# Queries and keys projected already transposed, in half-heads, in the attention part of a decoder layer

## The chip, the cores and the metric

The kernel runs on one core of a Trainium2 chip. The metric is the device time of one execution in microseconds. The kernel before takes 2218.97 us, the median of 3 runs (2217.65 to 2219.78).

## What is computed

A decoder layer on x of 16 batches, 256 positions, 512 features, in float32:

```python
x = x + attn(layernorm(x))      # 32 query heads of 64, 8 key/value heads, rotary
                                # embedding, causal window of 128, sinks, output projection
x = x + conv(ctx, ctx, layernorm(x))   # long convolution of k*v, 32 heads of 8 channels
x = x + mix(layernorm(x))       # sum of 8 factor matrices / sqrt(8), and a bias
```

Of the attention, what matters here:

```python
qkv = x @ qkv_w.T + qkv_b
q, k = rope(q), rope(k)         # [x1*cos - x2*sin, x2*cos + x1*sin], halves of 32
logits = einsum('bqhmd,bkhd->bhmqk', q, k) / 8     # masked: j > i or j <= i - 128
w = exp(logits - m) / (sum(exp(logits - m)) + exp(sink - m))
out = einsum('bhmqk,bkhd->bqhmd', w, v).reshape(...) @ out_w.T + out_b
```

## The kernel before, in words

Three parts follow each other: `attention_part`, `conv_part`, `mix_part`. Only the first is touched, with `rope_tables` and `layout`, which prepare its inputs.

The attention goes twice over the 16 batches, because the weights, each split in a high and a low float32r part so that three matmuls (high by high, low by high, high by low) stand for one in float32, fill SBUF for half of the key heads only. The first sweep takes key heads 0 to 3 and writes x plus its part of the output to DRAM (`part_dram`), the second takes 4 to 7, adds, and forms the second layernorm and its transpose (`q2_dram`) for the convolution. I call one batch in one sweep a window; there are 32. A window has eight slots: p % 4 names the key head (group), j the tile of 128 positions. A body is eight p's by two j's, so two windows; bodies 0, 1, 7, 8, 9, 15 and the drain 16 are written out, those between are loops. Nothing plans the order at run time: each engine's `body` issues its calls by p and j, with a lag for each stage, and semaphores tie the engines.

In slot (p, j), TensorE: transposes the four probability tiles of lag 3 into pP (`p_transposes`, L520); projects one tile of 128 positions onto the 384 columns of a group, queries, key and value together (`qkv`, L486, twelve matmuls into wP); transposes the rotated queries and keys of the slot two before (`q_transposes`, L496, three into tP); forms scores of two heads (`scores`, L510, heads of 64 rows in two halves of the array, into sP); probabilities by values (`pv`, L534, into vP); and the output projection of lag 5 (`out_projection`, L557, six matmuls of 512 columns into oP). Transposes of x (L465) and of the second layernorm (L566) share tP.

VectorE, in the order of its slot: `rotate` (L835, L836), the additions of the rotary embedding; `divide` (L861 to L869), which needs the exponentials of the slot before; `mask_transposed` (L878); `qkv_evac` (L826, L829), out of wP with the bias; `mask_min` (L846, L852), masks and row minimum of this slot's scores; low parts of x (`x_low`, L810) and of the output (`o_low`, L816); now and then layernorms and the residual (L893). ScalarE: `p_evac` (L657), `q_evac` (L636), `o_high` (L663), `exps` (L648, L651). POOL: the products of the rotary embedding (`cos_sin_parts`, L726, L730), the power for the layernorms (L720), the sinks (L740), without which L651 can't start, the bias to the residual (L764), and at the start the sum of the mix's factors by DMA (L770).

The split of the first sweep's weights goes with the start; that of the second's runs through body 0 and body 1 (L601, L924), its parts go to DRAM and are loaded at the turn between the sweeps. SP's queue carries all loads and stores in the order written.

Of the kernel before, what the change touches and what calls it, by code (L numbers as in the profile page):

```python
# [18 lines left out]
F32 = mybir.dt.float32  # L19
I32 = mybir.dt.int32  # L20
# [5 lines left out]
P = 128  # L26
# [7 lines left out]
GW = (QM + 2) * HD  # L34
RW = (QM + 1) * HD
SM_SCALE = 1.0 / math.sqrt(HD)
MASKED = 1.0e30
CHUNK = 2 * (QM + 2) * HD
# [12 lines left out]
def rope_tables():  # L51
# [14 lines left out]
    key = np.stack([np.concatenate([cos, cos], axis=1), np.concatenate([-sin, sin], axis=1)], axis=1)  # L66
    tab = np.stack([-SM_SCALE * key] * QM + [key], axis=2).astype(np.float32)
    return np.ascontiguousarray(tab.reshape(NT, P, 2 * (QM + 1) * HD).transpose(1, 0, 2))
# [18 lines left out]
def attention_part(nc, x, wqkv, bqkv, wout, bout, sinks, rope, masks, ident, factors, ssm_pad, dcoef,  # L87
                   x1_dram, q2_dram, pad_dram, fsum):

    part_dram = nc.dram_tensor("x_part_rows", [B, T, D], F32).ap()

    wq_dram = nc.dram_tensor("w_split", [GS, 2, P, KD * GW], F32).ap()
    xt_dram = nc.dram_tensor("xt_split", [B, 2, P, NT * KD * P], F32).ap()
    wo_dram = nc.dram_tensor("wo_split", [GS, 2, P, 2 * D], F32).ap()
    with ExitStack() as ctx:
# [8 lines left out]

        wh = sb("wh", [P, GS, KD, GW], F32R)
        wl = sb("wl", [P, GS, KD, GW], F32R)
        woh = sb("woh", [P, GS, 2, D], F32R)
        wol = sb("wol", [P, GS, 2, D], F32R)  # L120
        bias_sb = sb("bias_sb", [P, GS, GW])
        bo_sb = sb("bo_sb", [P, D])
        sink_sb = sb("sink_sb", [P, NH])
        rope_sb = sb("rope_sb", [P, NT, 2, QM + 1, HD])
# [4 lines left out]
        xTh = sb("xTh", [P, 2, NT, KD, P], F32R)  # L129
        xTl = sb("xTl", [P, 2, NT, KD, P], F32R)  # L130
# [5 lines left out]
        qk = sb("qk", [P, 2, QM + 1, HD])  # L136
        m1 = sb("m1", [P, 2, QM + 1, HD])
        m2 = sb("m2", [P, 2, QM + 1, HD])
        qr = sb("qr", [P, 2, QM + 2, HD])
        vv = sb("vv", [P, NKV, NT, HD])  # L140
        qT = sb("qT", [P, 2, 3, T])
# [5 lines left out]
        pT = sb("pT", [P, 2, 2, SK])  # L147
        den = sb("den", [P, 4, 2 * NT])
        rden = sb("rden", [P, 4, 2 * NT])
        oTh = sb("oTh", [P, 4, NT, 2, P], F32R)  # L150
        oTl = sb("oTl", [P, 4, NT, 2, P], F32R)
        xb = sb("xb", [P, NT, D])
        x1 = sb("x1", [P, NT, D])
        work = sb("work", [P, 3 * CHUNK])
        x1n = work[:, 0:NT * D].rearrange("p (t d) -> p t d", t=NT)
        x1T = work[:, NT * D:2 * NT * D].rearrange("p (c t) -> p c t", c=KD)
# [77 lines left out]
        def chunks(gs):  # L234
            return [("qkv", g, i) for g in gs for i in range(2)] + [("out", g, i) for g in gs for i in range(2)]
# [1173 lines left out]
```

## Time and profile before

| | us |
|---|---|
| median of 3 runs | 2218.97 (2217.65 to 2219.78) |
| the profiled execution, its own time | 2217.66 |
| its span | 2215.5 |
| TensorE busy | 2086.6 (94%) |
| VectorE busy | 1753.5 (79%) |
| ScalarE busy | 929.9 (42%) |
| POOL busy | 835.2 (38%) |
| attention, to the first transfer of the convolution | 1721.1 |

The span is from the first to the last instruction of the program. Busy times are unions over an engine's instructions; a matmul's recorded duration holds the way through the array, so that matmuls overlap in the record and the distance between two starts, not the duration, tells what one costs. Where a row of VectorE ends later than the next begins, the same holds.

### The profile page before, as it was taken

To read this page: it belongs to the slowest core of one execution; us is meant where nothing else is said; L and a number is where in the kernel's file an instruction comes from. 1 tells how busy PE (TensorE), PEld (TensorE's weight loads), DVE (VectorE), ACT (ScalarE), POOL (GpSimd) and SP (SyncE) were. 2 spreads that over 40 slices of the span, in tenths; PEclk is the share of its full clock that TensorE was granted. 3 is DMA by queue.
4 is the path that set the end of the run, shared out by engine and by line. 5 is a ranking of instruction groups with operands and counts; after the bars stand their busy time and mean duration, and the time that the engine had idled before them with its cause. 6 is when DMAs were issued, how large, how long until landed. Compare 5 with 4: busy or idle time off the path is not lost. (4 is left out here: it accounts for less than half of the span.)

```text
span 2215.5 us, 45127 instructions
## 1 busy us (share of the span) xinstructions
PE 2086.6 (94%) x12672; PEld 1656.8 (75%) x12672; DVE 1753.5 (79%) x6468; ACT 929.9 (42%) x3429; POOL 835.2 (38%) x1327
## 2 busy tenths in 40 slices
PE   5669999999999999999999999999998699999699
PEld 4557888888888888887777777777875577676587
DVE  6558887878888887777777787778776599999787
ACT  3334444444444444444444444444443122222233
POOL 3223333333344333333333333333331355454354
PEclk9889999999999999999999999999999899999899
DMA  7663111111111114311121111111101633233364
GB/s 232 187 188 116 49 61 55 64 60 48 48 48 48 48 65 180 115 39 49 50 76 49 49 48 49 61 54 48 49 30 48 231 84 90 83 91 83 111 219 160
DMA packets 84765, 191.72 MB, mean 87 GB/s; under 512 B 7777, under 2 KB 20833, under 8 KB 84465
## 3 DMA queue, kind: packets, MB, share of 16 engines
q1 hardware_dynamic: 72112, 157.67, 21.6%
q10 hardware_dynamic: 8640, 23.86, 2.9%
q0 software_dynamic: 3840, 8.39, 2.1%
q14 instruction: 126, 1.02, 0.1%
q8 instruction: 47, 0.77, 0.1%
HBM read 120.68 MB, written 60.90 MB: 82 GB/s over the span
## 5 line engine op out<-in xcount | busy, mean ns | idle before, releaser
L726 POOL TENSOR_TENSOR m<-qk,rope_sb 128x320 f32<-128x320 f32 x256 | 223.3, 872 | 956.9 <-DVE qk L826 956.9
L648 ACT ACTIVATE pr<-pr,mx 128x128 f32<-128x128 f32 x1024 | 399.3, 391 | 222.1 <-DVE mx L852 222.1
L486 PE MATMUL wP<-wh,xTh 128*128 128x384 f32 x1024 | 373.4, 365 | 10.5 <-DVE vv L829 10.5
L1091 PE MATMUL y<-kv,tap 128*128 128x288 f32 x1280 | 330.3, 414 | 27.3 <-DVE res L1139 9.6
L486 PE MATMUL wP<-wh,xTl 128*128 128x384 f32 x1024 | 353.3, 345 | 0.0
L486 PE MATMUL wP<-wl,xTh 128*128 128x384 f32 x1024 | 350.8, 343 | 0.0
L1091 PEld LDWEIGHTS y<-kv,tap 128*128 128x128 f32 x1280 | 240.6, 192 | 116.9 <-issue 25.1
L730 POOL TENSOR_TENSOR m<-qk,rope_sb 128x160 f32<-128x160 f32 x512 | 260.3, 530 | 0.0
L510 PE MATMUL sP<-qT 64*128 64x128 f32 (+1 forms) x2048 | 237.1, 350 | 1.0 <-DVE mx L852 1.0
L636 ACT COPY qT<-tP 128x384 f32<-128x384 f32 x256 | 122.6, 479 | 272.4 <-PE tP L496 272.0
L852 DVE CUSTOM_DVE_ANT_0 pr<-sP,mask_sb 128x128 f32<-128x128 f32 x1024 | 235.1, 284 | 0.7
L869 DVE TENSOR_SCALAR pr<-pr,rden 128x128 f32<-128x128 f32 x1024 | 224.0, 282 | 9.1
L557 PE MATMUL oP<-woh,oTh 128*128 128x512 f32 x512 | 229.6, 448 | 0.0
L534 PE MATMUL vP<-pT,vv 128*64 128x256 f32 (+1 forms) x2048 | 223.6, 339 | 0.4 <-DVE oTl L816 0.4
L1041 POOL TENSOR_TENSOR kv<-kk 128x1024 f32<-128x1024 f32 x64 | 144.1, 2251 | 182.8 <-PE y L1091 158.5
L534 PEld LDWEIGHTS vP<-pT,vv 128*64 128x64 f32 x2048 | 124.5, 136 | 115.5 <-issue 73.8
L486 PEld LDWEIGHTS wP<-wh,xTh 128*128 128x128 f32 x1024 | 197.6, 193 | 13.7 <-issue 11.8
L557 PE MATMUL oP<-wol,oTh 128*128 128x512 f32 x512 | 203.2, 397 | 0.0
L557 PE MATMUL oP<-woh,oTl 128*128 128x512 f32 x512 | 201.4, 393 | 0.0
L520 PE MATMUL pP<-id_sb,pr 128*128 128x128 f32 x1024 | 157.5, 277 | 45.4 <-DVE pT L878 42.3
L486 PEld LDWEIGHTS wP<-wh,xTl 128*128 128x128 f32 x1024 | 197.9, 193 | 0.0
L486 PEld LDWEIGHTS wP<-wl,xTh 128*128 128x128 f32 x1024 | 196.7, 192 | 0.0
(93 smaller groups left out, 3594.2 us busy)
## 6 DMA issues: line engine op xcount, KB each, us to landing
tap<-padded_taps SPq DMA_DIRECT2D x64, 256.0 KB, 3.4
kk<-in_ctxt SPq DMA_DIRECT2D x64, 192.0 KB, 3.1
x_in<-in_x SPq DMA_DIRECT2D x16, 512.0 KB, 4.9
fsum<-in_factors POOLq DMA_DIRECT2D x8, 1024.0 KB, 9.6
xb<-in_x SPq DMA_DIRECT2D x16, 512.0 KB, 4.3
xt_split<-xTh SPq DMA_DIRECT2D x16, 512.0 KB, 2.6
xt_split<-xTl SPq DMA_DIRECT2D x16, 512.0 KB, 3.7
x_part_rows<-x SPq DMA_DIRECT2D x16, 512.0 KB, 3.1
```

Source lines behind the costliest of these rows:

```text
L486: last = pe.matmul(wP[:, 0:GW], a[:, p // 4, j, c, :], w[:, g, c, :], start=(c == 0 and n == 0), stop=(c == KD - 1 and n == 2))
L510: last = pe.matmul(sP[:, a, k0:P + 2 * k0], qT[r, s, j, t * P:(t + 1) * P], qT[r, s, 2, 0:(t + 1) * P], start=True, stop=True)
L520: last = pe.transpose(pP[:, (2 * a + t) * P:(2 * a + t + 1) * P], pr[:, (2 * p + 2 + j) % 4, a, t * P:(t + 1) * P], id_sb[:])
L534: last = pe.matmul(vP[a * HD:(a + 1) * HD, k * P:T], vu[:, k, :], pT[:, s, a, 2 * k * P:2 * P + k * P], start=(k == 0), stop=(k == 1))
L557: last = pe.matmul(oP[j][:], a[:, (p - 5) % 4, j, c, :], w[:, g, c, :], start=(g == 0 and c == 0 and n == 0), stop=(g == GS - 1 and c == 1 ...
L648: act.activation(pr[:, s, a, cols], pr[:, s, a, cols], ACT.Exp, bias=mx[:, s, i:i + 1], scale=-1.0, accum_out=ac[:, s, i:i + 1])
L726: pool.tensor_tensor(m1[:, j], qk[:, j], rope_sb[:, j, 0], ALU.mult)
L730: last = pool.tensor_tensor(m2[:, j, :, d:d + half], qk[:, j, :, o:o + half], rope_sb[:, j, 1, :, d:d + half], ALU.mult)
L852: last = dve.tensor_tensor_reduce(pr[:, s, a, t * P:(t + 1) * P], sP[:, a, 2 * t * P:(2 * t + 1) * P], mask_sb[:, t * P:(t + 1) * P], 1.0, ...
L869: last = dve.tensor_scalar(pr[:, s, a, cols], pr[:, s, a, cols], rden[:, s, i:i + 1], None, ALU.mult)
L1041: pool.tensor_tensor(kv[:, s, :, 0:4 * n].rearrange("p c (d n) -> p c d n", d=4), k0.unsqueeze(2).broadcast_to([P, KD, 4, n]), shifted, AL ...
L1091: last = pe.matmul(y[:, s, c, 0:NY], tap[:, s, d * P:(d + 1) * P], kv[:, s, c - d, :], start=(d == 0), stop=(d == c))
```

## The change

Queries, keys and values of four key heads are projected in six units per window instead of eight calls per window: five units (`unit`, L499) hold the weights still and stream x, so that the result comes out transposed, 128 rows being one half (32 numbers) of four heads, 256 columns being the positions; one unit (L492) makes the values of all four heads. Units stand in slots 0, 1, 3, 5, 6 and 7. The transposes of queries and keys go, with tP.

VectorE multiplies each unit out of PSUM with cosine and sine, adding the bias on the way (`turned`, L791, four instructions of 128x256); POOL adds the two products (`rotate`, L700) into qT or kT. Scores are formed for one query head of each of four key heads at a time, in four groups of 32 rows, two half-heads accumulated (L514), once per p. A row of four heads is now one query head of each key head, and weights and sinks are reordered for it. The output projection runs in a window of its own, one to two windows behind, one tile after the other, into one bank (L560). The residual comes in slots 3 and 7. The second sweep's weights are split at the turn, out of DRAM into the places of the first's, ten chunks of 1024 columns (L610, L781), without going through DRAM. The factors are summed in body 1 instead of body 0. The buffer `work` goes; x_in and xn take its uses.

On TensorE, a slot with j = 0 in the loop of the first sweep; names in it are the tiles of the lists above, an `x2` counts instructions. Before, from the end of the projection on:

```order
L486 MATMUL wP<-wl,xTh 128x384
L496 MATMUL tP<-id_sb,qr 128x128 x3
L510 MATMUL sP<-qT 128x128 x2
L510 MATMUL sP<-qT 128x256 x2
L534 MATMUL vP<-pT,vv 64x256 x2
L534 MATMUL vP<-pT,vv 64x128 x2
L557 MATMUL oP<-woh,oTh 128x512
```

and with the change, from the end of a unit on:

```order
L499 MATMUL wP<-xTh,wl 128x256
L514 MATMUL sP<-kT,qT 128x128 x8
L514 MATMUL sP<-kT,qT 128x256 x8
L538 MATMUL vP<-pT,vv 64x256 x2
L538 MATMUL vP<-pT,vv 64x128 x2
L560 MATMUL oP<-woh,oTh 128x512
```

The transposes between projection and scores are gone; the scores of two slots stand together, in four times as many matmuls.

On VectorE, from one minimum to the next mask. Before, in a slot in which a low part of x follows:

```order
L852 ISA mx 128x1
L816 TENSOR_TENSOR oTl<-vP,oTh 128x2x128
L835 TENSOR_TENSOR qr<-m 128x256
L836 TENSOR_TENSOR qr<-m 128x128
L861 TENSOR_TENSOR den<-ac,es 128x4
L863 RECIPROCAL rden<-den 128x4
L869 TENSOR_SCALAR pr<-pr,rden 128x128 x4
L878 TENSOR_TENSOR pT<-pP,mask_sb 128x2x256
L826 TENSOR_TENSOR qk<-wP,bias_sb 128x320
L829 TENSOR_TENSOR vv<-wP,bias_sb 128x64
L846 COPY_PREDICATED sP<-mask_sb,sP 128x2x128
```

and with the change, at the turn, with a split in it:

```order
L815 ISA mx 128x1
L850 TENSOR_TENSOR oTl<-vP,oTh 128x256
L781 TENSOR_TENSOR wl<-x_in,wh 128x1024
L824 TENSOR_TENSOR den<-ac,es 128x4
L826 RECIPROCAL rden<-den 128x4
L832 TENSOR_SCALAR pr<-pr,rden 128x128 x4
L841 TENSOR_TENSOR pT<-pP,mask_sb 128x2x256
L791 SCALAR_TENSOR_TENSOR m<-wP,bqk_sb,rope_sb 128x256 x4
L809 COPY_PREDICATED sP<-mask_sb,sP 128x2x128
```

The additions left the stretch ahead of the division, and four instructions of 128x256 stand where two smaller ones stood, between the masked transposes and the next mask. The diff, cut:

```diff
...
@@ TensorE
+                steps = [(wh, xTh), (wh, xTl), (wl, xTh)]
+                if n == V_UNIT:
...
+                    for h in range(2):
+                        for c in range(KD):
+                            for i, (w, a) in enumerate(steps):
+                                last = pe.matmul(wP[:, h * T:(h + 1) * T], w[:, n, c, h * P:(h + 1) * P], a[:, s, c, :],
+                                                 start=(c == 0 and i == 0), stop=(c == KD - 1 and i == 2))
+                    last.then_inc(qk_done, 1)
...
-            def q_transposes(y, p, j):
...
                 for t in range(NT):
-                    for a in range(2):
-                        r = slice(a * HD, a * HD + HD)
-                        k0 = t * P
-                        last = pe.matmul(sP[:, a, k0:P + 2 * k0], qT[r, s, j, t * P:(t + 1) * P],
-                                         qT[r, s, 2, 0:(t + 1) * P], start=True, stop=True)
+                    for h in range(2):
+                        for r in range(GS):
+                            rr = slice(r * 32, r * 32 + 32)
+                            last = pe.matmul(sP[:, r, t * P:P + 2 * t * P], qT[rr, p % 2, h, t * P:(t + 1) * P],
+                                             kT[rr, kslot, h, 0:(t + 1) * P], start=(h == 0), stop=(h == 1))
...
                         if x_next(y, p, j):
+                            x_transposes(y.window(p) + 1, p % 4 - 1)
+                        elif x1_here(y, p, j):
...
+                        if j == 0 and y.here(p, 2):
+                            scores(y, p)
...
@@ POOL
-            def cos_sin_parts(y, p, j):
...
+                pool.tensor_tensor(dst, m1[:, s], m2[:, s], ALU.add).then_inc(qr_ready, 1)
...
@@ VectorE
+            def turned(y, p, i):
...
+                for dst, h, half, f in [(m1, 0, 0, 0), (m1, 1, 1, 0), (m2, 0, 1, 1), (m2, 1, 0, 2)]:
+                    last = dve.scalar_tensor_tensor(dst[:, s, h], wP[:, half * T:(half + 1) * T], bias[:, half:half + 1],
+                                                    tab[:, f], ALU.add, ALU.mult)
...
-                        u, jj = (p - 1, 1) if j == 0 else (p, 0)
-                        if y.here(u, 0):
-                            rotate(y, u, jj)
...
+                        if residual_tile(y, p, j) is not None:
+                            residual(y, p, residual_tile(y, p, j))
+                        n = unit_of(p, j)
...
+                                turned(y, p, rope_index(n))
+                        if x_next(y, p, j):
+                            x_low(y.window(p) + 1, (p // 4 + 1) % 2, p % 4 - 1)
                         if y.here(p, 2):
                             mask_min(y, p, j)
...
+                        for i, n in split_now(y, p, j):
+                            split_low(i, n)
...
```

## Rows read from the trace of the kernel before

**Rows 1.** Windows: stretch, length, busy us of each engine (instructions), granted clock, DMA.

```profile
191.60:792.60 601.00, 599.82 (x4010) 483.04 (x4009) 503.83 (x2150) 287.58 (x1175) 237.48 (x420) 1.00 0.17 57
```

**Rows 2.** Windows of L861 alone, one division per slot, counted by its x.

```profile
45.40:191.60 146.20, 2.47 (x16) 0.85 0.65 179
191.60:792.60 601.00, 16.30 (x96) 1.00 0.17 57
...
1092.10:1503.30 411.20, 10.33 (x64) 1.00 0.15 52
```

**Rows 3.** Timeline of TensorE, one slot: start us, duration us, instruction, count.

```profile
599.98 0.49 PE L496 MATMUL tP<-id_sb,qr 128*128 128x128 f32 x3
600.39 0.93 PE L510 MATMUL sP<-qT 64*128 64x128 f32 x8
601.25 0.87 PE L534 MATMUL vP<-pT,vv 128*64 128x256 f32 x8
...
602.62 0.39 PE L557 MATMUL oP<-wol,oTh 128*128 128x512 f32 x1
602.85 0.39 PE L557 MATMUL oP<-woh,oTh 128*128 128x512 f32 x1
...
604.35 0.33 PE L486 MATMUL wP<-wl,xTh 128*128 128x384 f32 x1
604.52 0.34 PE L486 MATMUL wP<-wh,xTh 128*128 128x384 f32 x1
...
606.10 0.27 PE L496 MATMUL tP<-id_sb,qr 128*128 128x128 f32 x1
```

**Rows 4.** Timeline of VectorE in the drain, from one division to the next.

```profile
1691.78 0.16 DVE L861 TENSOR_TENSOR den<-ac,es 128x4 f32<-128x4 f32 x1 [1.20 <-ACT es L651]
...
1692.98 0.68 DVE L878 TENSOR_TENSOR pT<-pP,mask_sb 128x512 f32<-128x512 f32 x1
1693.58 0.42 DVE L846 COPY_PREDICATED sP<-mask_sb,sP 128x256 f32<-128x256 int32 x1
...
1694.75 0.08 DVE L852 DVE_READ_ACCUMULATOR2_ANT mx<- 128x1 f32 x1
...
1696.65 0.16 DVE L861 TENSOR_TENSOR den<-ac,es 128x4 f32<-128x4 f32 x1 [0.56 <-ACT es L651]
```

**Rows 5.** Timeline of VectorE, an instruction out of PSUM and its follower.

```profile
602.67 0.42 DVE L816 TENSOR_TENSOR oTl<-vP,oTh 128x256 fp32r<-128x256 f32 x1
603.01 0.41 DVE L835 TENSOR_TENSOR qr<-m 128x256 f32<-128x256 f32 x1
```

**Rows 6.** Timeline, a division held by POOL's power.

```profile
615.38 0.08 DVE L852 DVE_READ_ACCUMULATOR2_ANT mx<- 128x1 f32 x1
...
618.94 0.16 DVE L861 TENSOR_TENSOR den<-ac,es 128x4 f32<-128x4 f32 x1 [0.80 <-ACT es L651]
```

**Rows 7.** Timeline, a division held by POOL's additions to xb.

```profile
609.10 2.73 POOL L764 TENSOR_TENSOR xb<-xb,bo_sb 128x512 f32<-128x512 f32 x2
...
610.59 1.39 DVE L836 TENSOR_TENSOR qr<-m 128x128 f32<-128x128 f32 x1
...
611.90 0.15 DVE L861 TENSOR_TENSOR den<-ac,es 128x4 f32<-128x4 f32 x1
```

**Rows 8.** Timeline of TensorE and windows, an idle stretch and the clock behind it.

```profile
123.86 0.45 PE L520 MATMUL pP<-id_sb,pr 128*128 128x128 f32 x1 [3.45 <-DVE pT L878]
...
123.50:127.00 3.50, 3.14 (x12) 3.17 (x13) 2.25 (x13) 1.55 (x8) 2.81 (x5) 0.54 0.63 201
```

**Rows 9.** Timeline of body 0, a low part of the second sweep's weights, and one cast.

```profile
64.80 0.96 DVE L924 TENSOR_TENSOR work<-work 128x768 fp32r<-128x768 f32 x1 [8.67 <-ACT work L601]
...
71.47 0.81 ACT L601 CAST work<-work 128x768 fp32r<-128x768 f32 x1
```

**Rows 10.** Timeline of SP, the convolution's first transfer.

```profile
1721.12 0.35 SPq L1023 DMA_DIRECT2D kk<-in_ctxt  x1
```

**Rows 11.** The page, costliest groups: count | busy us, mean ns of one.

```profile
L486 PEld LDWEIGHTS wP<-wh,xTl 128*128 128x128 f32 x1024 | 197.9, 193 | 0.0
```

More of the change, by code:

```diff
@@ new lines, in x1_transposes, with unit_free @@
+            def x1_transposes(r, t, roped):
+                n = 2 * (r - B) + t
+                pe.wait_ge(x1n_ready, n + 1)
+                pe.wait_ge(m_ready, roped)
+                wait(pe, x1t_evac, n)
+                for c in range(KD):
+                    last = pe.transpose(wP[:, c * P:(c + 1) * P], x1n[:, t, c * P:(c + 1) * P], id_sb[:])
+                last.then_inc(x1t_done, 1)
+            def unit_free(y, p, n):
+                v = y.window(p)
+                if n == 5:
+                    pe.wait_ge(v_ready, v + 1)
+                elif n == 0:
+                    wait(pe, m_ready, (QM + 1) * v)
+                else:
+                    pe.wait_ge(m_ready, (QM + 1) * v + n)
+                if n in (2, 3):
+                    if fresh(y, p):
+                        pe.wait_ge(xt_lo, 2 * v + n + 1)
+                    elif late(y, 3, p):
+                        pe.wait_ge(x1t_evac, 2 * (v - 3 - B) + n - 1)
@@ L551, in out_projection @@
-                if g == 0:
-                    wait(pe, x1_ready, 4 * y.m + 2 * ((p - 5) // 4) - 1 + j)
-                steps = [(oTh, woh), (oTl, woh), (oTh, wol)]
-                for c in range(2):
-                    for n, (a, w) in enumerate(steps):
-                        last = pe.matmul(oP[j][:], a[:, (p - 5) % 4, j, c, :], w[:, g, c, :],
-                                         start=(g == 0 and c == 0 and n == 0), stop=(g == GS - 1 and c == 1 and n == 2))
-                last.then_inc(out_done, 1)
@@ new lines, in out_projection, with out_here @@
+                if k == 0:
+                    wait(pe, x1_ready, 2 * v + t)
+                steps = [(oTh, woh), (oTl, woh), (oTh, wol)]
+                for c in (2 * k, 2 * k + 1):
+                    for n, (a, w) in enumerate(steps):
+                        last = pe.matmul(oP[:], a[:, o, c, t * P:(t + 1) * P], w[:, c, :],
+                                         start=(c == 0 and n == 0), stop=(c == NO - 1 and n == 2))
+                last.then_inc(out_done, 1)
+            def out_here(y, p, j):
+                last_slot = p % 4 == 3 and j == 1
+                if y.first:
+                    return p == 7 and j == 1
+                return not (y.drain and p == 7 and j == 1)
@@ L573, in body @@
+            for t in range(NT):
+                x_transposes(0, t)
             def body(y):
@@ L1351, in _, with decoder_layer @@
             steps(dve, body, lag=4)
[L1354 removed]
+def decoder_layer(nc, x, ctxt, wqkv, bqk, bv, wout, bout, sinks, ssm_pad, dcoef, factors, bias, rope, masks, ident, out):
     x1_dram = nc.dram_tensor("x1_rows", [B, T, D], F32).ap()
```

768 lines of the change are left out of this document (356 added, 412 removed).

## Prediction

> **What bounds the kernel now.** I read a table of windows first, then one slot on TensorE, then the drain. The reader is to see that TensorE is busy 599.8 of 601.0 us in the first sweep [rows 1]. VectorE's divisions (L861, one per slot) count the slots: 96 in 601.0 us and 64 in 411.2 us [rows 2]. Eight slots make a window, so a window takes 50.1 us in the first sweep and 51.4 in the second. The first 16 take 146.2 us, against 100 at the steady pace.
>
> One slot on TensorE [rows 3] runs from 599.98 to 606.10, 6.12 us, of which three query transposes take 0.41 and the scores 0.86. TensorE is the bound, but hardly: behind it lies a ring over VectorE and ScalarE. The exponentials of a slot need its mask and minimum (L852), the next slot's division needs them, and VectorE works in order, so that the next mask comes behind that division. The drain, where no projection is left, shows the bare ring [rows 4]: from one division to the next 4.87 us, of which 1.82 pass between the last minimum (1694.83) and the division, 1.20 are the division, 0.60 the masked transposes, 1.25 the mask and minimum.
>
> **The change part by part, TensorE.** Query transposes go: 0.41 x 8 = 3.3 us per window. Scores go from eight calls of 0.86 to four. One now does four rounds (two half-heads, two tiles); a matmul of 128 columns is two records of 0.107 us and one of 256 two of 0.218, worked out of those 0.86 (2 x 0.107 + 2 x 0.218 + 0.2 of filling and of changing shape). If four row groups run beside each other as two do now, four rounds are 1.3 + 0.2 = 1.5 us, 6.0 per window against 6.9; if only two do, 2.8 us, 11.2 per window. I take the four, for the eight records of now already show pairs beside each other.
>
> Projections keep their columns but become 144 matmuls of 256 instead of 96 of 384. The pitch is 0.17 us at 384 columns and 0.23 at 512 [rows 3]: columns at 2.4 GHz (0.160, 0.213) and some 0.016. For 256 that makes 0.123. The bounds are 0.107, the columns alone, and 0.175, no gain from fewer columns; the three transposes, each with a weight load and 0.107 apart by the records' lengths above, speak for the low side. So 17.7 us against 16.8. The output projection keeps its 48 matmuls. TensorE's sum per window: 49.0 + 1.1 (transposes of x) - 3.3 - 0.9 + 0.9 = 46.8, about 46.5 with four changes of shape fewer.
>
> **VectorE and its ring.** Out go the evacuation (0.52 per slot in the ring: 0.40 and 0.12) and the rotation's additions. Those lay while ScalarE did the exponentials, so their removal frees nothing. In comes, in five of eight slots and in the ring between masked transposes and mask, L791: four instructions of 128x256 out of PSUM. The nearest is L816, same size and also out of PSUM, 0.42 long, the next starting 0.34 after it [rows 5]; 4 x 0.34 = 1.35 us. The lower bound is 0.26 each, what 256 more elements add from L816 to the 128x512 of L878, also out of PSUM (0.60 to the next start [rows 4]), the upper 0.42 with no overlap: 1.0 to 1.7. The value unit costs 0.60, as L878. Two residual tiles (0.60 each) now stand before the mask instead of under the exponentials, so do the two low parts of x in the first sweep (0.60 each), and the second layernorm's start in the second (1.7).
>
> Two waits of POOL remain in the ring in the first sweep. The power for x's layernorm stands ahead of the sinks in POOL's queue: the division came 3.48 us after the minimum, 1.66 over the 1.82 [rows 6]. And while POOL adds the bias to xb (two adds, 2.73 us), VectorE's two-input instructions from SBUF stand still: L836 took 1.39, and the division came at 611.90, 3.03 after its minimum, 1.2 over the 1.82 [rows 7]. The new POOL addition of 128x512 (half of those 2.73) runs beside the mask and minimum, which come out of PSUM, and costs nothing; without that cover it would hold the division by its own length.
>
> Window, first sweep: 8 x 4.87 + 5 x 1.35 + 0.6 + 1.2 + 1.2 + 1.66 + 1.2 = **51.6**. Second: 8 x 4.87 + 5 x 1.35 + 0.6 + 1.2 + 1.7 = **49.2**, taken as 49.4, since TensorE is held once by VectorE's long last slot. Both stand above TensorE's 46.5: the ring becomes the bound, and most of what TensorE saves is lost. TensorE now idles. In slot 2 of a window of the first sweep it waits some 3 us for the normalised x, which comes only after slot 1's minimum. After such a gap, of 3.45 us, the granted clock of the next 3.5 us was 0.54 [rows 8], the lower level. Transposes and scores right behind it take 2 us longer, of which half fits in: + 0.9, so **52.5** in the first sweep.
>
> **Start, turn, end.** At the start each slot waited for the second sweep's weights, which went from DRAM through a split and out again: L924 once stood 8.67 us for its cast [rows 9]. These leave, and so does the summing of the factors by DMA, now in slots 16 to 31: 1 MB in two slots, 12.9 us, is 81 GB/s more than the sweep's 57 [rows 1], below the start's 179 [rows 2], so I take it as hidden. New, estimated: the first projection starts at some 13 us; 5 us at the lower clock, 1.4 for L791, 3.0 for the next unit, then on VectorE five splits (6), L791 twice (2.7), a layernorm (2.7), low parts (1.2), mask (1.3) and the exponentials (1.8) make the first division at about 39 us instead of 45.5. Three slots of some 8.4 with a split in each follow, then 8 of 6.1 and five of 6.8. The 17th division comes at about 147 instead of 191.7: **-45**. A split costs a slot 2.2 us: its cast on ScalarE (1.05 for 1024 elements, by the 0.81 of 768) comes behind the exponentials, VectorE's 1.14 after that (0.96 for 768, less the overlap), and only then the division. In SP's queue the turn's ten loads stand, each behind the split before, ahead of the store of x1 and the load of xb. Those have four slots, some 25 us, until VectorE asks for them in slot 3, so I put them at nothing; if a split came late, SP and with it the residual would wait as long.
>
> From there to the last division, before, 1505 us (191.7 to 1696.65). Now: 107 slots of the first sweep, 13.4 x 52.5 = 702, - 3 for the last window without an x, + 5 splits 11; 16 x 49.4 = 790, + 5 splits 11, - 3 for windows without a second layernorm; drain 25. Sum 1533: **+28**. End: the last minimum to the first transfer of the convolution was 26.3 us (1694.83 to 1721.12 [rows 10]); the output projection now lags by up to 11 slots instead of five, five calls of 1.5 less what already stood there: **+5**. Convolution and mix are not touched.
>
> -45 + 28 + 5 = -12. The profiled execution took 2217.7 us (span 2215.5), 1.3 below the median of the runs, 2219.0. So **2206 us**.
>
> **One rule against the trace.** The 0.39 us matmuls stand 0.23 apart and those of 384 columns 0.17 [rows 3], though each has a weight load, 0.193 on record [rows 11]: the loads are hidden. The Trainium skill (TensorE: Matmul & The Clock Gate, section The mechanism) says that a weight load overlaps matmuls in flight only where the row group differs. By that rule the trace does not agree: here the loads and the matmuls have the same full height and yet follow each other at the pitch of their columns. By the rows the sum stays 2206, by the rule it would be the 2464 of the rival below.
>
> **Rivals.**
> *TensorE stays the bound through small matmuls (ends slower).* Place: L492 and L499. At the other end of the bounds, 0.175 instead of 0.123, a window needs 46.5 + 7.5 = 54.0 us. It decides from 0.143 in the second sweep (49.4) and from 0.16 in the first. Result: 29.4 windows, + 1.5 x 13.4 + 4.6 x 16 = + 94: about 2300. *Exposed weight loads (slower still).* With each load, as long as the 128 columns of a transpose (0.107), ahead of its matmul instead of beside the one before, 144 x 0.214 make a window of 59.6 and a time of 2464. Against it: 384 columns and such a load would be 0.267 apart, and are 0.17. It is the rule of the page named above.
> *Scores run two at a time* (the change doesn't do what it says): + 5.2 per window on TensorE, 51.7: bound in the second sweep, + 2.3 x 16 = 37, late scores in the first + 10: 2253.
> *The start gives nothing or half,* because transfers are late behind each other in SP's queue, or the ring meets waits that I don't see: 2225 to 2250.
> *The ring is shorter than its rows say,* since instructions overlap more or the start gains more: 2150 to 2190. For: the ring stands on 1.82 us that ScalarE might cut. Against: its four exponentials have the same form after.
>
> **How the numbers follow.** What a measurement tells from no change is 0.2%, 4.4 us about 2219. Chances: ring as computed, 2185 to 2225, 0.56; small matmuls 0.10; exposed loads 0.02; scores in pairs 0.06; start or unseen waits 0.14; shorter ring 0.12. Faster: the last, and three quarters of the first, 0.54. Same (2214.5 to 2223.4): 0.13. Slower: 0.33. The range leaves out the upper half of the small-matmul case and the lower part of the short ring: 2165 to 2285.
>
> **What would show it.** Right: divisions 4.9 apart in slots without a unit and 6.2 in those with one; TensorE idle 8 to 12% in the sweeps, its waits ended by VectorE; VectorE's division ended by ScalarE nearly always; L499 pitch near 0.123; scores near 1.5 us; 17th division near 147 us. Wrong: TensorE without gaps (small matmuls or scores), or L791 over 0.42 us, or slots with waits for DMA.

## The result and the profile after

The changed kernel takes 2263.35 us (median of 4 runs, 2262.38 to 2264.49) against 2218.56 before (4 runs): ratio 1.0202, 95% interval 1.0184 to 1.0219. It is 2% slower. The forecast was 2206, faster, with a chance of 0.54 for faster and 0.33 for slower; the time lies in the range given, on the side of the smaller chance.

From the page of the changed kernel: the span, TensorE's and VectorE's busy time, then two of VectorE's groups (busy us, mean ns | idle time before them and what ended it).

```profile
span 2260.6 us, 48490 instructions
...
PE 2029.4 (90%) x15488; PEld 1634.3 (72%) x15488; DVE 1720.5 (76%) x6104; ACT 803.9 (36%) x3161; POOL 557.6 (25%) x719
...
L824 DVE TENSOR_TENSOR den<-ac,es 128x4 f32<-128x4 f32 x256 | 52.7, 206 | 343.9 <-ACT es L632 314.7
L791 DVE SCALAR_TENSOR_TENSOR m<-wP,bqk_sb,rope_sb 128x256 f32<-128x256 f32 x640 | 264.4, 476 | 19.5 <-PE wP L499 18.8
```

TensorE is busy 90% of the span. VectorE's division L824 stood 343.9 us idle before it, 314.7 of them until ScalarE's last exponential. By these waits the ring over VectorE and ScalarE is the bound, as forecast (E1 to E3 test it). What came out otherwise is its length.

VectorE's divisions in the stretches of the forecast, as in [rows 2] (stretch and length, busy us of the divisions and their number, granted clock, DMA share, GB/s); each stretch begins just before the division that opens it:

```profile
46.30:154.45 108.15, 3.40 (x16) 0.91 0.22 63
154.45:880.80 726.35, 26.05 (x107) 0.96 0.22 64
880.80:1709.50 828.70, 22.47 (x128) 0.99 0.15 51
```

| stretch | before | forecast | now |
|---|---|---|---|
| to the first division | 45.5 | 39 | 46.4 |
| first to 17th | 146.2 | 108 | 108.1 |
| 17th to 124th | | 710 | 726.4 |
| 124th to 252nd | | 798 | 828.7 |
| 252nd to last (256th) | | 25 | 20.1 |
| 17th to last | 1505.0 | 1533 | 1575.2 |
| last division to the span's end | 518.9 | 523.9 | 530.9 |

So 37 us were won at the start, 70 lost between the 17th and the last division, 12 at the end: +45.

One slot on VectorE, the last of a window (slot 7) in the first sweep, to be read against the drain's bare one [rows 4] (start, length, engine, line, operation):

```profile
600.43 0.16 DVE L824 TENSOR_TENSOR den<-ac,es 128x4 f32<-128x4 f32 x1 [1.48 <-ACT es L632]
...
601.63 0.69 DVE L841 TENSOR_TENSOR pT<-pP,mask_sb 128x512 f32<-128x512 f32 x1
602.24 0.68 DVE L863 TENSOR_TENSOR x<-oP,xb 128x512 f32<-128x512 f32 x1
602.83 1.65 DVE L791 SCALAR_TENSOR_TENSOR m<-wP,bqk_sb,rope_sb 128x256 f32<-128x256 f32 x4
604.40 0.42 DVE L809 COPY_PREDICATED sP<-mask_sb,sP 128x256 f32<-128x256 int32 x1
...
605.57 0.42 DVE L850 TENSOR_TENSOR oTl<-vP,oTh 128x256 fp32r<-128x256 f32 x1
607.47 0.16 DVE L824 TENSOR_TENSOR den<-ac,es 128x4 f32<-128x4 f32 x1 [1.48 <-ACT es L632]
```

From division to division 7.04 us, where the drain has 4.87: the residual takes 0.59 (602.24 to 602.83) and L791's four products 1.57 (602.83 to 604.40), all of it between the masked transposes and the mask. Then the same wait of 1.48 us for the exponentials. By such rows a window of the first sweep is 7.97 + 6.44 + 5.47 + 7.85 + 5.47 + 6.44 + 5.47 + 7.04 = 52.15 us (slots 0 to 7) and one of the second 6.44 + 6.44 + 4.87 + 7.03 + 4.87 + 6.44 + 5.47 + 9.13 = 50.7; forecast were 51.6 and 49.2. On top, slot 2 of the first sweep took up to 6.75, and eight slots took 1.9 to 2.5 us beyond these.

These eight are where the two loops of five bodies branch back. VectorE's waits up to the last division (in total, times, longest), then one such place: VectorE's last row before the branch and first behind it, and ScalarE's exponentials of the sinks, which the division waits for.

```profile
DVE den L824 <- ACT es L632: 314.7, 234, 1.5
DVE den L824 <- issue: 29.2, 8, 3.9
```
```profile
1294.93 0.42 DVE L850 TENSOR_TENSOR oTl<-vP,oTh 128x256 fp32r<-128x256 f32 x1
1298.70 0.16 DVE L824 TENSOR_TENSOR den<-ac,es 128x4 f32<-128x4 f32 x1 [3.35 <-issue]
```
```profile
1296.60 0.19 ACT L632 ACTIVATE es<-sk 128x4 f32<-128x4 f32 x1
```

The exponentials are there at 1296.79 (1296.60 + 0.19), the division starts at 1298.70, 1.9 us later, with nothing on record that held it. At the eight branches back it was late by 2.11, 2.06, 2.30, 2.11, 2.27, 1.91, 2.49 and 2.46 us, 17.7 in all; everywhere else in a steady window the difference is 0.02 to 0.04.

### The profile page after: what moved, and what is told of

Read it like the earlier page. It is cut to its first block and busy times, and to the rows that moved or that the text cites. A ratio compares the mean times of both kernels' runs of the same rounds, so it can differ in the third digit from the quotient of the medians.

```text
span 2260.6 us, 48490 instructions
## 1 busy us (share of the span) xinstructions
PE 2029.4 (90%) x15488; PEld 1634.3 (72%) x15488; DVE 1720.5 (76%) x6104; ACT 803.9 (36%) x3161; POOL 557.6 (25%) x719
## 3 DMA queue, kind: packets, MB, share of 16 engines
q8 instruction: 129, 2.11, 0.4%
## 5 line engine op out<-in xcount | busy, mean ns | idle before, releaser
L499 PE MATMUL wP<-xTh,wh 128*128 128x256 f32 x1280 | 382.5, 299 | 20.8 <-DVE m L791 16.9
L499 PE MATMUL wP<-xTl,wh 128*128 128x256 f32 x1280 | 368.3, 288 | 0.0
L499 PE MATMUL wP<-xTh,wl 128*128 128x256 f32 x1280 | 367.1, 287 | 0.0
L700 POOL TENSOR_TENSOR qT<-m 128x512 f32<-128x512 f32 x128 | 164.8, 1287 | 690.9 <-DVE m L791 690.9
L824 DVE TENSOR_TENSOR den<-ac,es 128x4 f32<-128x4 f32 x256 | 52.7, 206 | 343.9 <-ACT es L632 314.7
L791 DVE SCALAR_TENSOR_TENSOR m<-wP,bqk_sb,rope_sb 128x256 f32<-128x256 f32 x640 | 264.4, 476 | 19.5 <-PE wP L499 18.8
L499 PEld LDWEIGHTS wP<-xTh,wh 128*128 128x128 f32 x1280 | 250.6, 196 | 26.7 <-DVE m L791 11.3
L560 PE MATMUL oP<-woh,oTh 128*128 128x512 f32 x512 | 231.2, 451 | 34.6 <-DVE x L863 34.4
L499 PEld LDWEIGHTS wP<-xTl,wh 128*128 128x128 f32 x1280 | 250.8, 196 | 0.0
L499 PEld LDWEIGHTS wP<-xTh,wl 128*128 128x128 f32 x1280 | 250.4, 196 | 0.0
L514 PE MATMUL sP<-kT,qT 32*128 32x128 f32 (+1 forms) x4096 | 221.5, 356 | 20.0 <-DVE mx L815 19.8
L560 PE MATMUL oP<-wol,oTh 128*128 128x512 f32 x512 | 204.1, 399 | 0.0
L560 PE MATMUL oP<-woh,oTl 128*128 128x512 f32 x512 | 204.0, 398 | 0.0
L514 PEld LDWEIGHTS sP<-kT,qT 32*128 32x128 f32 x4096 | 162.6, 199 | 47.0 <-issue 20.2
```

Of the source, the lines that this page charges most:

```text
L499: last = pe.matmul(wP[:, h * T:(h + 1) * T], w[:, n, c, h * P:(h + 1) * P], a[:, s, c, :], start=(c == 0 and i == 0), stop=(c == KD - 1 an ...
L514: last = pe.matmul(sP[:, r, t * P:P + 2 * t * P], qT[rr, p % 2, h, t * P:(t + 1) * P], kT[rr, kslot, h, 0:(t + 1) * P], start=(h == 0), st ...
L560: last = pe.matmul(oP[:], a[:, o, c, t * P:(t + 1) * P], w[:, c, :], start=(c == 0 and n == 0), stop=(c == NO - 1 and n == 2))
L700: pool.tensor_tensor(dst, m1[:, s], m2[:, s], ALU.add).then_inc(qr_ready, 1)
L791: last = dve.scalar_tensor_tensor(dst[:, s, h], wP[:, half * T:(half + 1) * T], bias[:, half:half + 1], tab[:, f], ALU.add, ALU.mult)
```

## The experiments

All times are medians, set against the changed kernel's 2263.35 unless said otherwise. Each kernel is the changed one but for the edit shown.

### E1 and E2: more work on VectorE, inside the ring and outside

```diff
 # E1, in turned()
+                last = dve.scalar_tensor_tensor(spare[:, s], wP[:, 0:T], bias[:, 0:1], tab[:, 2], ALU.add, ALU.mult)
                 last.then_inc(m_ready, 1)
 # E2, in o_low(), behind the masks
+                for i in range(2):
+                    dve.tensor_tensor(spare[:, j, i], vP[:, 0:T], oTh[:, (u // 4) % 2, c].bitcast(F32), ALU.subtract)
```

> One product more of the rotation (L791's form, 128x256 from PSUM, into a spare tile) in each of the five query and key units of a window, ahead of the masks as the others are. Ring theory (VectorE and ScalarE hand the same slot to each other, and the rotation stands inside that ring): every one costs its start to start of 0.39 us, 160 units = about +62 us against the changed kernel's 2263, so 2325, and the slots with a unit of queries or keys grow from 6.44 to 6.83. TensorE theory (its own work sets the pace): within 10 us of 2263.

> Two 128x256 subtractions more in every slot (256 slots, 0.34 us each, 174 us of VectorE work in all), put behind the masks, where VectorE waits for the exponentials. Ring theory: hidden in a wait of 1.2 to 1.5 us; only slot 0 of a window of sweep 1, where the layernorm's power and with it the sinks come later, pays some 0.7, so 0 to +12 us: 2263 to 2275. Theory that VectorE is full (its sum of work is the bound): +120 to +174 us. TensorE theory: within 10 us of 2263, so that this run alone does not tell it from the ring.

E1: 2322.94 us, **+60** for 160 instructions, 0.37 each; its unit slots are 6.83 us. E2: 2286.80, **+23** for 512 instructions. So an instruction ahead of the masks costs all but its full distance of 0.39, one behind them 0.05. VectorE's sum of work is not the bound; the place is. E2 was dearer than expected (up to 12): at the 113th division it is 24.8 us behind, at the 241st 26.6, so the first sweep pays nearly all of it. There slot 0 is 8.63 instead of 7.97 (as expected, the layernorm and its power come later), and slot 2 up to 7.4 instead of 6.75: TensorE idles 3.5 to 4.4 us in slot 1 instead of 2.1 to 3.0, and in 11 of 12 windows the granted clock of slot 2 is 0.58 to 0.78.

### E3: less work on TensorE

```diff
-                steps = [(wh, xTh), (wh, xTl), (wl, xTh)]
+                steps = [(wh, xTh), (wh, xTl)]
```

> Leaves out the third pass of the projection of queries, keys and values (low weights times high x): 48 of the 144 products of a window, so the outputs lack the low part of the weights. TensorE has 5.8 us less in each of 32 windows. Ring theory: the pace does not change; only at the eight loop-backs, where TensorE comes late, and at the start may 5 to 20 us go: 2243 to 2260. TensorE theory: -5.8 x 32 = -186 us, 2080.

2253.48 us, **-10**, of which 4.2 are the first division (42.2 instead of 46.4). The five looped bodies of the first sweep, of the changed kernel and of E3 (columns: stretch and its length, busy us of TensorE, its weight loads, VectorE, ScalarE, GpSimd, granted clock, DMA share, GB/s):

```profile
260.60:802.90 542.30, 492.99 (x4242) 403.44 (x4240) 408.31 (x1680) 201.73 (x901) 109.94 (x160) 0.96 0.14 49
```
```profile
256.70:794.40 537.70, 450.15 (x3760) 350.63 (x3760) 407.37 (x1681) 200.03 (x901) 110.01 (x160) 0.93 0.15 49
```

TensorE sheds 42.8 us of busy time (492.99 to 450.15) and the stretch 4.6. The granted clock fell too, 0.96 to 0.93, which lengthens what is left. TensorE does not set the pace: that theory asked for -186.

### E7: the sinks ahead of the layernorm's power

GpSimd's two steps change places in the program; nothing else.

> GpSimd takes the sinks ahead of the layernorm's power in the slot in which it has both; nothing else. Ring theory: slot 0 of every window of sweep 1 goes from 7.97 to 6.44 us (as in sweep 2, where there is no such power): 15 x 1.5 = -23 us, 2238 to 2245. If the slot is held by TensorE: 2263.

2240.18 us, **-23**. Slot 0 of the first sweep is 6.65 instead of 7.97, but for two slots behind a branch back, and slot 2, up to 6.75 in the changed kernel, is 5.46 to 5.91. Of the forecast's term for this wait, 1.66, slot 0 gives back 1.3 (it stood 1.5 over the 6.44 of the second sweep).

### E8 and E10: no branches back

```diff
-            with eng.Fori(2, HM - 1) as m:
+            for m in range(2, HM - 1):
                 body(Body(m, 0))
```
and the same for the second loop, in the changed kernel (E8) and in the kernel before (E10).

> The two loops of five bodies written out, so that no engine branches back. At each of the eight branches back VectorE's division came 1.9 to 2.5 us after its exponential sum, and in sweep 1 TensorE was late behind it by another 0 to 4 us. If the branch is the cause: -8 x 2.2 - 8 = -18 to -27 us, 2236 to 2246. If it is something else that falls at the end of a body (a layernorm, a DMA): 2263.

> The kernel before the change with its two loops of five bodies written out. Theory that the branch back was there all along: its looped bodies took 100.4 and 102.8 us, the written-out ones beside them 98.4 and 101.1, so 8 x 1.8 = -14 us, 2202 to 2208. Theory that only the changed kernel pays for it (a longer body): 2219.

E8: 2235.98 us, **-27**, the far end of what was expected (24.3 between the two profiled executions). Its bodies 2 to 6 all take 105.8 to 105.9 us (106.0 to 111.7 with the loop), bodies 10 to 13 of the second sweep 101.2 to 101.6 (103.7 to 104.0): besides VectorE's 17.7 us, TensorE came late behind the branch in the first sweep (slot 0 there takes up to 11.98 instead of 7.97). E10: 2216.93 against 2219.07, ratio 0.9992 (0.9983 to 1.0002): **nothing**. My reading of the longer looped bodies of before as the branch's price was wrong. The divisions of before around one branch back in the second sweep, then the same ones written out:

```profile
1257.08 0.16 DVE L861 TENSOR_TENSOR den<-ac,es 128x4 f32<-128x4 f32 x1 [0.68 <-ACT es L651]
...
1268.33 0.15 DVE L861 TENSOR_TENSOR den<-ac,es 128x4 f32<-128x4 f32 x1
...
1273.72 0.16 DVE L861 TENSOR_TENSOR den<-ac,es 128x4 f32<-128x4 f32 x1 [0.44 <-ACT es L651]
...
1279.12 0.16 DVE L861 TENSOR_TENSOR den<-ac,es 128x4 f32<-128x4 f32 x1 [0.35 <-ACT es L651]
...
1286.88 0.16 DVE L861 TENSOR_TENSOR den<-ac,es 128x4 f32<-128x4 f32 x1 [0.78 <-ACT es L651]
...
1292.29 0.15 DVE L861 TENSOR_TENSOR den<-ac,es 128x4 f32<-128x4 f32 x1
```
```profile
1257.23 0.16 DVE L861 TENSOR_TENSOR den<-ac,es 128x4 f32<-128x4 f32 x1 [0.68 <-ACT es L651]
...
1265.08 0.16 DVE L861 TENSOR_TENSOR den<-ac,es 128x4 f32<-128x4 f32 x1 [0.94 <-ACT es L651]
...
1271.22 0.16 DVE L861 TENSOR_TENSOR den<-ac,es 128x4 f32<-128x4 f32 x1 [0.94 <-ACT es L651]
...
1277.35 0.16 DVE L861 TENSOR_TENSOR den<-ac,es 128x4 f32<-128x4 f32 x1 [0.35 <-ACT es L651]
...
1285.86 0.16 DVE L861 TENSOR_TENSOR den<-ac,es 128x4 f32<-128x4 f32 x1 [0.78 <-ACT es L651]
...
1291.48 0.16 DVE L861 TENSOR_TENSOR den<-ac,es 128x4 f32<-128x4 f32 x1
```

The branch is there in the kernel before: one slot takes 11.25 us instead of 7.85. But the next four take 5.39, 5.40, 7.76 and 5.41 instead of 6.14, 6.13, 8.51 and 5.62. VectorE catches up with TensorE, and 1.0 us of 3.4 is left (35.2 against 34.25 in five slots). Where the ring is the bound, nothing can be caught up. Writing the loops out removes the branch together with all else that a loop brings; the runs don't tell these apart.

### E9: what the fused form costs

```diff
-                    last = dve.scalar_tensor_tensor(dst[:, s, h], wP[:, half * T:(half + 1) * T], bias[:, half:half + 1],
-                                                    tab[:, f], ALU.add, ALU.mult)
+                    last = dve.tensor_tensor(dst[:, s, h], wP[:, half * T:(half + 1) * T], tab[:, f], ALU.mult)
```

> The rotation's four products of a unit as plain two-input multiplications of the same 128x256 out of PSUM, without the addition of the bias (the bias of queries and keys is left out of the computation). This is the form by which the prediction priced L791 (0.34 us start to start). Ring theory, with the fused form as the dearer one: slots of queries and keys go from 6.44 to 6.24, 5 x 0.2 in each of 31 windows, -31 us, 2228 to 2238. If the price is of the place (PSUM, the half that is read) and not of the form: 2263.

2218.02 us, **-45**, level with the kernel before (ratio 0.9997, 0.9987 to 1.0006). The rows of L791 in the changed kernel and in E9 (duration min/median/max in ns):

```profile
L791 DVE SCALAR_TENSOR_TENSOR m<-wP,bqk_sb,rope_sb x640: 471/476/486, 19.1 to 1706.1; 128x256 f32<-128x256 f32 x160
```
```profile
L791 DVE TENSOR_TENSOR m<-wP,rope_sb x640: 410/417/426, 18.8 to 1663.9; 128x256 f32<-128x256 f32 x160
```

That is more than the 31 expected. 476 ns become 417, and start to start 0.392 become 0.331; unit slots go from 6.44 to 6.19, 160 x 0.25 = 39 us. Another 3 come at the first division (43.3). L816's 0.42 and 0.34, from which the forecast priced L791, are those of the plain form: right for it, wrong for the fused one.

### E12: the factors summed early again

The condition on GpSimd's factor DMAs goes back from body 1 to the first body.

> The changed kernel with the factors summed by DMA in slots 0 to 15 again, as before the change, instead of 16 to 31. If the start's gain (the 17th division 37 us earlier than before) came from this move, it goes back by 10 us or more: 2275 to 2300. If it came from the second sweep's weights alone, which no longer pass through DRAM there, within 5 us: 2258 to 2268.

2262.93 us, **no difference**; its 17th division is at 154.4 us, as now (154.5). The 37 us at the start do not hang on these DMAs. Of the start's moves that the forecast named, what is left is the second sweep's weights, no longer split there; this was not undone by itself, so that it is argued and not shown.

### E4 to E6, E13, E14: taking the rotation out of the ring

```diff
 # VectorE, in each slot (E4, E5, E13, E14)
-                        turned(y, p, rope_index(n)) or v_evac(y, p)
                         x_low(...)
                         mask_min(y, p, j)
+                        turned(y, p, rope_index(n)) or v_evac(y, p)
 # TensorE (E5, E6, E14)
+                        if j == 0 and y.here(p, 2):
+                            scores(y, p)
                         p_transposes(y, p, j)
                         unit(y, p, n)
-                        if j == 0 and y.here(p, 2):
-                            scores(y, p)
 # GpSimd (E5, E13): the unit of the slot before, behind this slot's division
+                                pool.wait_ge(pn_ready, 16 * y.m + 2 * u + jj + 1)
+                            rotate(y, q // 2, rope_index(n))
```

> VectorE's rotation of a unit and the value units' addition stand behind the masks of the same slot instead of ahead of them, under the wait for the exponentials, and GpSimd's addition of the rotated halves behind the sinks; no instruction more or less. Ring theory: five times 1.57 - 0.2 and 0.6 leave the ring of every window, and TensorE's 46.5 us becomes the bound: 52.15 to 46.5 in sweep 1, 50.7 to 46.5 in sweep 2, about -150 us if nothing else comes up, so 2110 to 2180. TensorE theory: within 10 us of 2263. Theory of late units (the units' results now reach TensorE 1.5 us later and that is what it waits for): 2263 or slower.

Not said there: E4 has the sinks ahead of the power too, as E7 and as E5, E13 and E14. E4: 2294.43 us, **+31**. Slower is what only the theory of late units allowed, but its cause is not there: TensorE never waits for the rotated halves. It does wait longer until L791 has emptied the units' bank, 43.3 us instead of 16.9 ahead of L499, but E13 below has 39.5 of that and is 84 us faster. Two other things are new. First, from E4, two rows under the exponentials and the first of the next division on VectorE, then GpSimd's addition:

```profile
652.35 1.66 DVE L791 SCALAR_TENSOR_TENSOR m<-wP,bqk_sb,rope_sb 128x256 f32<-128x256 f32 x4
653.92 0.42 DVE L850 TENSOR_TENSOR oTl<-vP,oTh 128x256 fp32r<-128x256 f32 x1
654.43 0.94 DVE L824 TENSOR_TENSOR den<-ac,es 128x4 f32<-128x4 f32 x1
```
```profile
654.08 1.27 POOL L700 TENSOR_TENSOR qT<-m 128x512 f32<-128x512 f32 x1 [1.37 <-DVE m L791]
```

The first operation of the division, 128x4, takes 0.94 us instead of 0.16: it ends at 655.37, where the addition ends (654.08 + 1.27). The Trainium skill (SBUF — State Buffer, section Who interferes with whom) says that a VectorE instruction with two inputs in SBUF and a GpSimd one that reads SBUF exclude each other, the later waiting for the whole of the earlier; the trace agrees. Behind a rotation ahead of the masks the addition ran beside instructions out of PSUM (604.64 to 605.93 in the changed kernel, beside L809 at 604.40, which took its usual 0.42) and held nothing, as the forecast had it with the words "without that cover it would hold the division by its own length". Second, from E4, slot 6: division, end of TensorE's unit, the scores, the mask.

```profile
610.41 1.22 DVE L824 TENSOR_TENSOR den<-ac,es 128x4 f32<-128x4 f32 x1
...
613.04 0.28 PE L492 MATMUL wP<-wl,xTh 128*128 128x256 f32 x1
...
613.25 1.59 PE L514 MATMUL sP<-kT,qT 32*128 32x128 f32 x32
...
615.06 0.43 DVE L809 COPY_PREDICATED sP<-mask_sb,sP 128x256 f32<-128x256 int32 x1 [1.71 <-PE sP L514]
```

VectorE waits 1.71 us for scores that TensorE gave only behind a whole unit; in the changed kernel L791 or the value's addition of that slot had covered this. Slot 6 takes 7.7 us, slot 0 9.5 in the first sweep (the text of E5 gives 7.7 for both). Four versions take away one, the other or both; the last, E6, stands outside the square:

> E4 with its two new waits taken away: on TensorE a pair's scores stand first in their slot instead of behind a unit (E4's slots 0 and 6 of a window were 7.7 us, transposes + unit + scores between the division and the masks), and GpSimd adds the rotated halves one slot later, behind the division (E4's first operation of the division took 0.94 instead of 0.16 us beside that addition), and the sinks ahead of the layernorm's power. Ring theory: nothing but the masks is left between division and exponentials, so the ring is 4.87 to 5.5 us in a slot, below TensorE's mean of 5.8, and TensorE's 46.5 us in a window is the bound: 2263 - 5.6 x 15 - 4.2 x 15 = 2115, range 2080 to 2160. TensorE theory (TensorE's own chain already bounds the changed kernel): above 2240.

> Only the scores moved to the head of their slot on TensorE, VectorE and GpSimd as in the changed kernel. Ring theory: the scores were ready before the masks asked for them (VectorE never waited there), so nothing, 2255 to 2266, and what there is comes from the stretches behind a loop-back in sweep 1. Theory that scores are late: -30 us or more.

> E4 (rotation behind the masks, sinks ahead of the power) with GpSimd's addition of the halves one slot later, but the scores where the change has them, behind the unit. If the addition beside the division cost E4 its gain: E4's 2294 less 0.78 in five slots of each of 31 windows, -120, 2175. If the scores behind the unit did: slots 0 and 6 stay at 7.7 and more, since there TensorE's chain and not VectorE's division is the longest, and only the other slots gain: about -50 to -70, 2225 to 2245.

> E4 with the scores at the head of their slot, but GpSimd's addition in the slot of its unit, beside the division. If the scores behind the unit cost E4 its gain: slots 0 and 6 fall from 7.7 to the 5.7 of the others with a held division, 2 x 2.0 x 31 = -124, 2170. If both count about alike: 2200 to 2230.

| rotation behind the masks, with | scores behind the unit | scores first |
|---|---|---|
| addition beside the division | 2294.43 (E4) | 2191.17 (E14) |
| addition one slot later | 2210.27 (E13) | 2140.13 (E5) |

The late addition alone gains 84, the scores alone 103, both 154. Slot 6 of the first sweep is 7.7 in E4, 7.5 in E13, 6.1 to 6.7 in E14 and 6.65 in E5. Both waits count, and about alike: E14 lies between its two cases (2170 and 2200 to 2230), nearer the one in which both count alike, and so does E13 (2175 and 2225 to 2245). E5 is inside its range, 25 over the 2115. E5 is 3.6% faster than the kernel before (ratio 0.9642, 0.9626 to 0.9658).

E6, the scores first with the rotation left ahead of the masks: 2383.06 us, **+120**. I expected nothing, since VectorE never waited for scores. My reading now is that their 1.6 us stand ahead of the unit, and that in that order VectorE needs the unit before it can mask. From its VectorE waits:

```profile
DVE m L791 <- PE wP L499: 56.1, 30, 4.2
DVE vv L799 <- PE wP L492: 46.2, 31, 2.4
```

In the changed kernel VectorE waited 18.8 us for L499 before L791. So TensorE's unit is now in the ring as well. The same move is worth -103 (E4 to E14) behind a rotation that lies under the exponentials, and +120 without it.

### E11: the fastest version

E5 with both loops written out.

> E5 with its loops written out too. Branch theory: its looped bodies took 97.3 to 102.7 us, the written-out ones beside them 97.4 (first sweep) and 95.9 (second), so 3.8 in each of five of the first and 1.9 in each of five of the second, about -22 to -28 us: 2112 to 2118.

2117.25 us, as expected, ratio to the kernel before 0.9544 (0.9528 to 0.956): **4.6% faster than before**, 6.5% than the changed kernel. VectorE's wait for the exponentials in E11, then four bodies of the second sweep in the changed kernel and in E11 (columns as in E3):

```profile
DVE den L828 <- ACT es L632: 138.7, 109, 1.5
```
```profile
1121.20:1536.50 415.30, 383.57 (x3394) 315.41 (x3393) 311.98 (x1328) 159.41 (x721) 67.60 (x112) 0.99 0.15 52
```
```profile
1020.40:1404.80 384.40, 378.14 (x3394) 309.96 (x3394) 313.22 (x1328) 163.86 (x722) 69.53 (x112) 1.00 0.16 56
```

The wait is 138.7 us, from 314.7. TensorE is busy 378.14 of 384.40 us, 98%, where it was 383.57 of 415.30, 92%: by these shares it is the bound again. A window takes 48.0 us there and 48.7 in the first sweep, 1.5 and 2.2 over TensorE's 46.5 of the forecast.

## Why the prediction was wrong, point by point

**TensorE's sum, right within 2%.** In E11 TensorE is busy 47.3 us a window (378.14/8 in the second sweep) at a granted clock of 1.00, for 46.5 forecast. Products of 256 columns start 0.12 apart (forecast 0.123, bounds 0.107 and 0.175), four row groups of scores run beside each other (32 records in 1.59 us, forecast 1.5), and TensorE idles by 8.7% in the first sweep and 7.6% in the second (forecast 8 to 12). The small matmuls, the exposed loads and the scores in pairs did not come. On the Trainium skill's rule that the forecast weighed (TensorE: Matmul & The Clock Gate, section The mechanism), the trace again does not agree: each of these products has a weight load of 0.19 us over the same 128 rows, more than the distance to the next product. The section's opening also lets a load into the background weight buffer go ahead of matmuls in flight; that fits, though no run here shows which it is.

**The ring as bound, right; its length, wrong.** The step that failed is the term "4 x 0.34 = 1.35 us". L791 measures 4 x 0.392 = 1.57, inside the bounds 1.0 to 1.7 but not the value taken; at 0.476 it also shows the forecast's own sign of being wrong, "L791 over 0.42 us". I took L816 as the nearest row since size and source were the same, and passed over that its form was not: L816 has two inputs and one operation, L791 a third input, the bias, and two operations. 160 units x 0.22 = 35 us. E1 and E9 show this price and that it is paid in full.

**The second failing step is one that was left out.** The ring's 4.87 came from the drain, where no loop branches back. E8 puts the branches at 27 us. The trace of before had them, slots of 11.15 to 11.48 us in the second sweep, but I summed windows of TensorE there, and by TensorE they cost next to nothing (E10: 2 us).

The sum of the misses, by the profiled executions: the start 7; between the 17th and the last division L791 32 (147 of the 160 units lie there), the branches 24 (E8), the second layernorm's start 6 (slot 7 of the second sweep is 9.13, so that it costs 2.1 and not 1.7); the end 7. Against them the drain 5, the additions to xb 5 and the power 2 (13.4 windows each), the clock 4, and 3 for the 0.2 that the forecast put on each window of the second sweep (49.4 for 49.2). That is 57, the distance between 2206 and 2263. Of these only L791 and the branches were taken out by a run; the others are read from slots, and that they add up so exactly is partly luck. E8 and E9 taken off by their measured amounts would give 2263 - 27 - 45 = 2191; the two were not run together.

**The clock's +0.9 per window, right in kind.** From two windows of the changed kernel, the transposes of x behind TensorE's idle stretch in slot 1, and the scores behind them:

```profile
293.17 0.63 PE L447 MATMUL wP<-id_sb,xn 128*128 128x128 f32 x4 [2.99 <-DVE xn L761]
293.73 1.59 PE L514 MATMUL sP<-kT,qT 32*128 32x128 f32 x32
```
```profile
402.03 1.09 PE L447 MATMUL wP<-id_sb,xn 128*128 128x128 f32 x4 [2.99 <-DVE xn L761]
403.04 2.94 PE L514 MATMUL sP<-kT,qT 32*128 32x128 f32 x32
```

The wait for the normalised x is 2.99 us in both. In the first window the granted clock of slot 2 is 1.00, the scores take 1.59 us and the slot 5.47; in the second they are 0.62 (0.50 during the scores, the lower level), 2.94 and 6.75. Of the 12 windows of bodies 1 to 6 three have 1.00 and 5.47 us, the other nine 0.60 to 0.78 and 5.80 to 6.75. So it is the clock that lengthens slot 2, by 0.56 on average instead of 0.9, some 8 us for 12. What decides between windows with the same wait is not shown. In E7 TensorE's idle time in slot 1 is mostly 1.7 us instead of 3, and 7 of the 12 windows have 1.00 and 5.47, the other five 0.70 or 0.71 and 5.61 to 5.91. The power (1.5 for 1.66 forecast) stood; the additions to xb cost 0.8, not 1.2.

**Start.** First division 46.4 instead of 39, though the 16 slots behind it took the 108 forecast. I priced one unit at the lower clock (5 us) and the next at the higher (3). Three stretches of the changed kernel (stretch and length, busy us of TensorE, its weight loads, VectorE, ScalarE, GpSimd, granted clock, DMA share, GB/s):

```profile
20.90:22.30 1.40, 1.38 (x12) 1.40 (x12) 1.25 (x4) 0.00 (x0) 1.24 (x1) 1.00 1.07 425
22.30:25.00 2.70, 2.70 (x15) 2.66 (x13) 1.35 (x3) 0.00 (x0) 1.62 (x1) 0.50 0.59 241
30.80:36.20 5.40, 5.38 (x24) 5.17 (x24) 0.99 (x1) 0.00 (x0) 0.00 (x0) 0.52 0.58 190
```

TensorE stood 1.96 us for L791 ahead of the second unit, began it at 20.92 at a granted clock of 1.00 (12 products in 1.40 us), and from 22.3 on has 0.50, the lower of the two levels (1.2 GHz), with products 0.21 apart (24.20, 24.42, 24.63). The third unit, behind another wait of 2.57 us, runs its whole 5.4 us at 0.52. The first unit (13.5 to 18.9) has the same 0.21, as I had it, though the granted clock of that stretch reads 1.00; new are 24 x 0.09 = 2.2 us for the third and 1.1 for half of the second. Another 2.1 are a sixth split, where I had counted five: VectorE stood 2.75 us for its cast (L781, at 45.21), so that the first division comes 3.9 us after its minimum and not 1.8. Some 2 are left, which I put down to the waits between the units on the one accumulator.

**Turn.** As forecast in kind: slots 8.5 with a split, 2.1 more than 6.44.

**End.** +12 instead of +5. The last division, the last window's two residuals, and the hand-over to the convolution:

```profile
1729.63 0.16 DVE L824 TENSOR_TENSOR den<-ac,es 128x4 f32<-128x4 f32 x1 [1.47 <-ACT es L632]
```
```profile
1746.76 0.69 DVE L863 TENSOR_TENSOR x<-oP,xb 128x512 f32<-128x512 f32 x1 [2.76 <-issue]
...
1753.89 0.69 DVE L863 TENSOR_TENSOR x<-oP,xb 128x512 f32<-128x512 f32 x1 [6.44 <-PE oP L560]
...
1764.61 0.35 SPq L978 DMA_DIRECT2D kk<-in_ctxt  x1
```

From the last division to the last residual 24.3 us (before 13.7, 1696.65 to 1710.38); from there to the convolution's first transfer both take the same 10.7, and 1.6 of the 12 come behind that. Eleven calls of the output projection lie between division and residual where six did, five more of 1.4 us = 7. I counted five more than before too, but subtracted "what already stood there", though all six still do. Of the 3.6 beyond those 7, TensorE's waits for the residual to empty the one bank are 1.8 (0.93 and 0.84); the rest stays open.

**The rivals.** Those on the slower side were TensorE or the start; the one with "waits that I don't see" (0.14) touches the branches, but ends at 2250. None said "the ring is longer than its rows", only "shorter". That was the error of the chances: the ring's own bounds (L791 from 1.0 to 1.7) reached 1.75 us a window above my sum, 2206 + 0.35 x 160 = 2262, and that side had no case.

## What to carry to other kernels

When a change moves the bound from one engine to a ring of two, price every instruction that lands inside the ring by a row of the same form (inputs and operations, not only size and source), and add the stalls that the old bound had absorbed, such as a branch back: they come due on the engine that now sets the pace. Then ask of each instruction in the ring whether its place is needed: here the order alone was worth 123 us (the sinks, which by themselves gave 23 in E7, moved with it). The rotation moved with neither scores nor a late addition lost 31 us (E4) and the scores moved alone 120 (E6); the rotation with one of the two gained 53 or 72 (E13, E14), with both 123.

## What the runs showed of the hardware that I had not expected

At a branch back VectorE's next instruction comes 1.9 to 2.5 us after the release of its wait (eight of eight), and in the first sweep TensorE is up to 4 us late behind it; written out, no such gap is left, and 27 us go. Behind the same wait of 2.99 us TensorE's granted clock was 1.00 over one slot and 0.62 over another. The fused product with a bias (128x256 out of PSUM) takes 476 ns, the plain one 417: the third input and second operation cost 0.06 us per instruction although they add no elements. What inside the chip makes any of these is not shown by these runs.
